# One raw mask buffer in each mask chain, and two places for its additions, in an eight-core two-layer kernel

## The chip, the cores and the metric

The kernel runs on the 8 cores of one Trainium2 chip. Each core works on its own 2048 of the 16384 tokens; the cores exchange nothing, and each reads the whole of the weights and of the mask. The metric is the device time in microseconds of the slowest core. Lower is better.

## The reference

x has shape (2, 8192, 4096). Both weights are 4096 by 4096, and the mask is 4096 by 4096 of int32.

```python
block_mask = mask.reshape(128, 32, 128, 32).astype(float32).sum(axis=(1, 3)) > 0
elem_mask  = repeat(repeat(block_mask, 32, axis=0), 32, axis=1)
x = x + layernorm(einsum('bsk,nk->bsn', layernorm(x), w1 * elem_mask))
x = x + layernorm(einsum('bsi,oi->bso', layernorm(x), sign(w2)) + bias)
```

So the 64 MB mask is reduced to one bit for each block of 32 by 32 weights, and these bits decide which blocks of the first weight matrix count.

## The kernel before

**Chunks and layers.** A core's 2048 tokens are worked on in four chunks (c = 0 to 3) of 512, each in 4 tiles of 128. For each chunk both layers follow one another. Each layer is 16 weight slabs (sl = 0 to 15): slab sl holds half of the contraction (kh = sl % 2) for 512 output features (nsl = sl // 2), 16 pieces of 128 by 512. TensorE multiplies a slab with 64 matmuls into 4 PSUM banks (line 456), and after each odd slab the result is copied out to ARAW.

**The first chunk prepares the weights.** Only in chunk 0 the float32 weights are read, eight pieces of 512 KB for each slab, by SyncE's queue into the two staging buffers WST (line 346). In layer 0 VectorE multiplies each piece with the block bits BTE and writes it as bfloat16 to the slab buffer WSL (line 375). In layer 1 ScalarE takes the sign (line 389). Each finished slab, 2 MB, is written by a DMA of GpSimd's queue to a cache in HBM (c1m and c2m, line 400). The chunks 1 to 3 read the slabs from these caches.

**The mask chain.** `emit_mask_chain(nsl, first)` makes the bits for the two slabs of one nsl; it runs 8 times, all in chunk 0. It has these steps:

- GpSimd (POOL) issues four loads of 128 rows of the mask, 2 MB each (line 230). The numbers of the rows run on over all chains, and even ones go to OS (the output buffer, not in use yet), odd ones to the first half of XP (a buffer that is used after layer 0). Load r + 1 is issued before the wait for load r.
- For each load it adds neighbours pairwise five times (line 250): 2048, 1024, 512, 256 and 128 sums for each partition, the large one out of OS or XP, all of them into the scratch tile MHI. After each addition it waits for its own semaphore. The last 128 sums of each r go to their own part of MHI, at 3072 and up.
- ScalarE converts these 4 x 128 sums into COLRED (line 264), TensorE sums over 32 partitions with a small matmul (line 274), VectorE compares with zero (line 288), TensorE transposes, and VectorE copies the bits into BT (line 292).
- GpSimd writes BT to HBM (line 305) and reads it back, spread over the partitions, into BTE with four DMAs (line 314).

**The order around it.** All engines run their instructions in the order in which the program emits them. The chains 0 and 1 stand ahead of the statistics of the first activation tiles. In layer 0 of chunk 0 the order for each sl is: the load and masking of slab sl + 1 (with the cache write on GpSimd, which waits for the masking), the matmuls of slab sl, and, when sl is even, the chain sl // 2 + 2. So on VectorE the comparison of chain 2 stands behind the masking of slab 1 and ahead of that of slab 2, and chain 3 stands between slabs 3 and 4.

Of the kernel before, what the change touches and what calls it, by code (L numbers as in the profile page):

```python
# [16 lines left out]
I32 = mybir.dt.int32  # L17
AF = mybir.ActivationFunctionType
# [19 lines left out]
def build():  # L38
# [5 lines left out]
    mask_d = nc.dram_tensor("mask", [D, D], I32, kind="ExternalInput")  # L44
# [10 lines left out]
    with es:  # L55
        def sb(name, shape, dt):
            return es.enter_context(nc.sbuf_tensor(name, shape, dt))
# [4 lines left out]
        XP = sb("XP", [128, NT * D], BF16)  # L62
# [4 lines left out]
        MHI = sb("MHI", [128, 3584], I32)  # L67
        COLRED = sb("COLRED", [128, 512], BF16)
# [17 lines left out]
        sem = {n: es.enter_context(nc.semaphore(n)) for n in SEMS}  # L86
        cnt = {n: 0 for n in SEMS}

        def inc(ins, n, k=1):
            cnt[n] += k  # L90
            ins.then_inc(sem[n], k)
            return (n, cnt[n])

        def wt(eng, marker):
            if marker is None:
                return
            n, v = marker
            if v > 0:
                eng.wait_ge(sem[n], v)
# [3 lines left out]
        OSi32 = OS[:, :].bitcast(I32)  # L103
# [112 lines left out]

        def emit_mask_chain(nsl, first):
            halv = {}

            @blk.gpsimd  # L220
            def _(g):
                stg = [OSi32, XP[:, 0:8192].bitcast(I32)]
                ld = {}

                def issue(r):
                    rt = nsl * 4 + r
                    if rt == 0:
                        wt(g, bias_os_free)
                    sn = "sM" if rt % 2 == 0 else "sM1"
                    g.dma_start(stg[rt % 2][:, 0:4096],  # L230
                                mask_d[rt * 128:(rt + 1) * 128, :]
                                ).then_inc(sem[sn], 16)
                    cnt[sn] += 16
                    ld[r] = (sn, cnt[sn])

                issue(0)
                for r in range(4):
                    rt = nsl * 4 + r
                    if r + 1 < 4:
                        issue(r + 1)  # L240
                    wt(g, ld[r])
                    if r == 0 and nsl > 0:
                        g.wait_ge(sem["vAs"], nsl)
                    spans = [(0, 2048), (2048, 1024), (0, 512), (2048, 256),
                             (3072 + r * 128, 128)]
                    cur = stg[rt % 2][:, 0:4096]
                    for hstep in range(5):
                        dst_off, dst_n = spans[hstep]
                        a = cur.rearrange("p (a two) -> p a two", two=2)
                        ins = g.tensor_tensor(MHI[:, dst_off:dst_off + dst_n],  # L250
                                              a[:, :, 0], a[:, :, 1], op=OP.add)
                        m = inc(ins, "vPs", 1)
                        g.wait_ge(sem["vPs"], m[1])
                        cur = MHI[:, dst_off:dst_off + dst_n]
                halv[nsl] = ("vPs", cnt["vPs"])

            conv = {}

            @blk.scalar
            def _(s):  # L260
                wt(s, halv[nsl])
                if nsl >= 1:
                    s.wait_ge(sem["vTp"], 5 * (nsl - 1) + 1)
                ins = s.activation(COLRED[:, :], MHI[:, 3072:3584], AF.Identity)  # L264
                conv[nsl] = inc(ins, "vAs", 1)

            @blk.tensor
            def _(t):
                wt(t, conv[nsl])
                if first:  # L270
                    wt(t, bias_ptB_free)
                if nsl >= 1:
                    t.wait_ge(sem["vMk"], 2 * (nsl - 1) + 1)
                ins = t.matmul(ptB[0:4, 0:512], P4T[:, :], COLRED[:, :],  # L274
                               start=True, stop=True)
                inc(ins, "vTp", 1)
                t.wait_ge(sem["vMk"], 2 * nsl + 1)
                for r in range(4):
                    ins = t.transpose(ptB[:, :].bitcast(BF16)[:, 1024 + r * 4:
                                                              1028 + r * 4],  # L280
                                      BRT[0:4, r * 128:(r + 1) * 128],
                                      IDN[0:4, 0:4])
                    inc(ins, "vTp", 1)

            @blk.vector
            def _(v):
                v.wait_ge(sem["vTp"], 5 * nsl + 1)
                ins = v.tensor_scalar(BRT[0:4, :], ptB[0:4, 0:512], 0.0, None,  # L288
                                      OP.is_gt)
                inc(ins, "vMk", 1)  # L290
                v.wait_ge(sem["vTp"], 5 * nsl + 5)
                ins = v.tensor_copy(BT[:, 16 * nsl:16 * nsl + 16],
                                    ptB[:, :].bitcast(BF16)[:, 1024:1040])
                inc(ins, "vMk", 1)

            res = {}

            @blk.gpsimd
            def _(g):
                g.wait_ge(sem["vMk"], 2 * nsl + 2)  # L300
                g.wait_ge(sem["sB"], cnt["sB"])
                if nsl >= 2:
                    wt(g, bte_freed[nsl - 2])
                bteb = BTE[nsl % 2]
                g.dma_start(btd_d[:, :], BT[:, 16 * nsl:16 * nsl + 16]
                            ).then_inc(sem["sB"], 16)
                cnt["sB"] += 16
                g.wait_ge(sem["sB"], cnt["sB"])
                for a in range(4):
                    out_ap = bass.AP(bteb[:, :].tensor, 32 * a * 512,  # L310
                                     [[512, 32], [16, 32], [1, 16]])
                    in_ap = bass.AP(btd_d[:, :].tensor, a * 16,
                                    [[0, 32], [64, 32], [1, 16]])
                    g.dma_start(out_ap, in_ap).then_inc(sem["sB"], 16)
                    cnt["sB"] += 16
                res["m"] = ("sB", cnt["sB"])

            bte_ready[nsl] = res["m"]
# [469 lines left out]
        for c in range(NCH):  # L788
            t0 = c * TC
            if c == 0:  # L790
                emit_p0_part1(0, list(range(NT)), phase="loads")
                emit_mask_chain(0, True)
                emit_mask_chain(1, False)
                emit_p0_part1(0, list(range(NT)), phase="stats")
            else:
                emit_p0_part1(c, [1, 2, 3])
# [3 lines left out]
            for layer in range(2):  # L800
# [21 lines left out]
                for sl in range(NSL):  # L822
                    if sl + 1 < NSL:
                        nxt = emit_w_load_prep(c, layer, sl + 1)
                    if layer == 0 and fin_pending[0] is not None:
                        fc, fev = fin_pending[0]
                        if sl == 0:
                            fin_chain[0] = emit_finalize_chain(fc, fev)
                        elif sl == 1:
                            for ftt in range(NT):  # L830
                                emit_finalize_tile(fc, fin_chain[0], ftt)
                            fin_pending[0] = None
                    ready, su = pend
                    emit_slab_mm(c, layer, sl, ready, su, ev_at, ht_mark, site,
                                 pre_tt=pre_tt if sl == 0 else None)
                    if c == 0 and layer == 0 and sl % 2 == 0 and sl // 2 + 2 <= 7:
                        emit_mask_chain(sl // 2 + 2, False)
                    if layer == 1 and sl == 8 and c + 1 < NCH:
                        emit_p0_part1(c + 1, [0])
                    if sl + 1 < NSL:  # L840
                        pend = nxt
# [52 lines left out]
```

## Time and profile before

| what | value |
|---|---|
| median of 3 runs (lowest to highest) | 3411.86 us (3408.38 to 3417.56) |
| the profiled execution's own time | 3400.95 us |
| its span, core 2, the slowest | 3399.4 us |
| spans of all cores | 3362.9 to 3399.4 us |
| mean granted TensorE clock, core 2 | 0.818 |
| busy: TensorE matmul, VectorE, ScalarE, GpSimd | 59%, 24%, 18%, 10% |
| share of POOL in the chain of work that ended last | 8% |
| additions of the mask tree, 32 large and 128 small | 115 us and 125.9 us |
| DMA on GpSimd's queue, on SyncE's queue | 194.08 MB, 377.51 MB |

The span is the time from the first to the last instruction of the slowest core in one profiled execution. A share of busy time is a mean over the whole span, although the kernel has stages with different limits: GpSimd's work lies all before about 1000 us, the matmul-heavy chunks 1 to 3 behind it. A chain of work that ended last is followed back from the last instruction, at each step to what released it.

### The profile page before, as it was taken

The numbers are of one execution on the slowest core, as the hardware profiler recorded it, in microseconds if no ns is written. First come the engines' busy times: TensorE is split into PE (matmuls) and PEld (weight loads), VectorE is DVE, ScalarE is ACT, GpSimd is POOL, SyncE is SP. The second block draws the span as 40 slices with busy tenths as digits, with TensorE's granted clock in tenths as the row PEclk, the third lists the DMA queues.
The fourth block names the chain that finished last, engine by engine and source line by source line (L and its number), as shares of the span: only waits on it lengthen the run. The fifth ranks groups of instructions, "written<-read, shape, count | busy, mean of one in ns | idle before, by whom it ended". The sixth has DMA issues, their size and how long they took to land.

```text
span 3399.4 us, 24072 instructions; the slowest of 8 cores (3362.9 to 3399.4 us)
## 1 busy us (share of the span) xinstructions
PE 2016.0 (59%) x9091; PEld 934.2 (27%) x9272; DVE 806.5 (24%) x1300; ACT 607.4 (18%) x460; POOL 343.1 (10%) x328
## 2 busy tenths in 40 slices
PE   1033113332524555555894799579569966965992
PEld 0011001110212222222342344234234432433441
DVE  0132112221440111024013222320222142022214
ACT  0120000000044333332114200301340030115000
POOL 4404432244000000000000000000000000000000
PEclk9986566665866777777997899789779978987996
DMA  3465556555734777664444343443424444342442
GB/s 124 130 205 195 192 210 224 184 187 184 232 133 161 228 230 234 228 217 149 173 152 146 117 180 149 149 173 149 148 107 159 181 149 173 149 148 75 153 160 108
DMA packets 72946, 573.14 MB, mean 169 GB/s; under 512 B 8800, under 2 KB 8816, under 8 KB 42112
## 3 DMA queue, kind: packets, MB, share of 16 engines
q1 hardware_dynamic: 54144, 377.51, 32.6%
q0 software_dynamic: 18688, 194.08, 15.9%
q8 instruction: 75, 1.23, 0.1%
q14 instruction: 39, 0.32, 0.0%
HBM read 470.86 MB, written 100.70 MB: 168 GB/s over the span
## 4 chain that ended last, share of the span: by engine, by line
PE 38%; DMA 28%; DVE 11%; ACT 10%; POOL 8%; issue 5%; DVEq 0%; SPq 0%; POOLq 0%; ACTq 0%
PE pmm L456 36%; DMA WST<-w2s 10%; DMA WST<-w1s 8%; POOL MHI L250 7%; DMA OS<-mask 3%; DMA out<-OS 3%; DVE WSL L375 2%; ACT WSL L389 2%; DMA XS<-x 2%; ACT HS L720 2%; ACT HS L689 2%; DVE OS L768 2%; ACT HT L214 1%; DVE BNST L575 1%; PE ptA L204 1%
## 5 line engine op out<-in xcount | busy, mean ns | idle before, releaser
L456 PE MATMUL pmm<-WSL,HT 128*128 128x512 bf16 x8011 | 1886.5, 397 | 446.3 <-ACT WSL L389 202.0
L456 PEld LDWEIGHTS pmm<-WSL,HT 128*128 128x128 bf16 x8192 | 826.3, 101 | 1497.2 <-issue 617.6
L512 DVE TENSOR_TENSOR ARAW<-pmm,BIASF 128x512 bf16<-128x512 f32 x128 | 88.3, 692 | 898.5 <-PE pmm L456 898.5
L274 PE MATMUL ptB<-COLRED,P4T 128*4 128x512 bf16 x8 | 4.7, 586 | 499.6 <-ACT COLRED L264 499.6
L204 PE MATMUL ptA<-IDN,HS 128*128 128x128 bf16 x576 | 64.7, 302 | 351.4 <-ACT HS L720 236.4
L375 DVE TENSOR_TENSOR WSL<-WST,BTE 128x1024 bf16<-128x1024 f32 x128 | 155.6, 1224 | 208.6 <-DMA WST<-w1s 207.1
L493 DVE BATCH_NORM_STATS2 BNST<-ARAW 128x6 f32<-128x512 bf16 x96 | 59.3, 680 | 533.8 <-ACT ARAW L483 533.8
L389 ACT ACTIVATE WSL<-WST 128x1024 bf16<-128x1024 f32 x128 | 134.7, 1056 | 258.8 <-DMA WST<-w2s 258.5
L204 PEld LDWEIGHTS ptA<-IDN,HS 128*128 128x128 bf16 x576 | 56.6, 140 | 364.7 <-issue 364.0
L264 ACT ACT_TABLE_LOAD x8 | 10.3, 1283 | 741.5 <-POOL MHI L250 741.5
L274 PEld LDWEIGHTS ptB<-COLRED,P4T 128*4 128x4 bf16 x8 | 0.6, 80 | 504.0 <-issue 504.0
L250 POOL TENSOR_TENSOR MHI<-MHI 128x1024 int32<-128x1024 int32 (+3 forms) x128 | 125.9, 984 | 18.3
L657 POOL DMA_DIRECT2D XS<-x x32 | 22.5, 703 | 1016.5 <-DVE XP L682 948.3
L214 ACT ACTIVATE HT<-ptA 128x2048 bf16<-128x2048 bf16 x36 | 67.6, 1877 | 274.2 <-PE ptA L204 274.2
L575 DVE BATCH_NORM_STATS2 BNST<-XS 128x6 f32<-128x512 f32 x128 | 78.4, 679 | 149.2 <-DMA XS<-x 149.2
L288 DVE TENSOR_SCALAR BRT<-ptB 4x512 bf16<-4x512 f32 x8 | 5.4, 679 | 433.7 <-PE ptB L274 433.7
L483 ACT ACTIVATE ARAW<-pmm 128x512 bf16<-128x512 f32 x96 | 57.3, 597 | 269.7 <-PE pmm L456 153.1
L483 ACT ACT_TABLE_LOAD x24 | 30.8, 1283 | 394.6 <-PE pmm L456 394.6
L519 DVE BATCH_NORM_STATS2 BNST<-ARAW 128x6 f32<-128x512 bf16 x160 | 98.9, 681 | 4.1
L544 POOL DMA_DIRECT2D XS<-x x24 | 12.7, 528 | 612.5 <-ACT HS L609 563.0
L768 DVE SCALAR_TENSOR_TENSOR OS<-XP,AUX,OS 128x4096 f32<-128x4096 bf16 x16 | 71.8, 4485 | 1.7
L250 POOL TENSOR_TENSOR MHI<-OS 128x2048 int32<-128x2048 int32 x16 | 57.6, 3601 | 109.6 <-DMA OS<-mask 109.5
(58 smaller groups left out, 807.7 us busy)
## 6 DMA issues: line engine op xcount, KB each, us to landing
WSL<-c1m SPq DMA_DIRECT2D x48, 2048.0 KB, 8.0
WSL<-c2m SPq DMA_DIRECT2D x48, 2048.0 KB, 8.0
WST<-w1s SPq DMA_DIRECT2D x128, 512.0 KB, 5.0
WST<-w2s SPq DMA_DIRECT2D x128, 512.0 KB, 4.7
XS<-x POOLq DMA_DIRECT2D x56, 1024.0 KB, 6.3
OS<-mask POOLq DMA_DIRECT2D x16, 2048.0 KB, 10.3
XP<-mask POOLq DMA_DIRECT2D x16, 2048.0 KB, 12.4
c1m<-WSL POOLq DMA_DIRECT2D x16, 2048.0 KB, 10.3
```

Of the source, the lines that this page charges most:

```text
L204: ins = t.transpose(pt[:, j * 128:(j + 1) * 128], HS[:, ktg * 128:(ktg + 1) * 128], IDN[:, :])
L214: ins = eng.activation(dst, src, AF.Identity)
L250: ins = g.tensor_tensor(MHI[:, dst_off:dst_off + dst_n], a[:, :, 0], a[:, :, 1], op=OP.add)
L375: ins = v.tensor_tensor(dst, src, mk, op=OP.mult)
L389: ins = s.activation(buf[:, j0 * 512:(j0 + KTQ) * 512], WST[(wfirst + q) % 2][:, :], AF.Sign)
L456: ins = t.matmul(acc_bank(use8, nsl, tt), st_ap, mv_ap, start=(kh == 0 and j == 0), stop=(kh == 1 and j == KTS - 1))
L483: ins = s.activation(dst, acc_bank(use8, nsl, tt), AF.Identity)
L512: ins = v.tensor_tensor(dst, acc_bank(use8, nsl, tt), BIASF[:, nsl * 512:(nsl + 1) * 512], op=OP.add)
L519: ins = v.bn_stats(BNST[:, sslot * 48 + nsl * 6: sslot * 48 + (nsl + 1) * 6], ARAW[:, tt * D + nsl * 512: tt * D + (nsl + 1) * 512])
L575: ins = v.bn_stats(bn[:, (hf * 4 + q) * 6: (hf * 4 + q + 1) * 6], xb[:, q * 512:(q + 1) * 512])
L689: ins = s.activation(HS[:, :], XP[:, tt * D:(tt + 1) * D], AF.Square, accum_out=XSQ[:, tt:tt + 1])
L768: ins = v.scalar_tensor_tensor(OS[:, :], XP[:, tt * D:(tt + 1) * D], mrs3, OS[:, :], OP.subtract, OP.add)
```

## The change

Within one chain all four loads now go to the same raw buffer: OS for even nsl, the first half of XP for odd nsl. A load is issued after the first (large) addition of the row block before it has finished, no longer before the wait for it. The sums of odd chains go to the second half of XP, and those of even chains to MHI. GpSimd's wait for ScalarE's conversion is for that of two chains before, and starts with chain 2. Sizes and number of all loads and additions are the same.

```diff
--- before.py
+++ after.py
@@ -216,42 +216,49 @@
 
         def emit_mask_chain(nsl, first):
             halv = {}
+            par = nsl % 2
+            XPI = XP[:, :].bitcast(I32)
+            if par == 0:
+                raw = OSi32[:, 0:4096]
+                tree = MHI
+                fin_base = 3072
+            else:
+                raw = XPI[:, 0:4096]
+                tree = XPI[:, 4096:8192]
+                fin_base = 3072
+            spans_tpl = [(0, 2048), (2048, 1024), (0, 512), (2048, 256)]
 
             @blk.gpsimd
             def _(g):
-                stg = [OSi32, XP[:, 0:8192].bitcast(I32)]
                 ld = {}
 
                 def issue(r):
                     rt = nsl * 4 + r
                     if rt == 0:
                         wt(g, bias_os_free)
-                    sn = "sM" if rt % 2 == 0 else "sM1"
-                    g.dma_start(stg[rt % 2][:, 0:4096],
-                                mask_d[rt * 128:(rt + 1) * 128, :]
+                    sn = "sM" if par == 0 else "sM1"
+                    g.dma_start(raw, mask_d[rt * 128:(rt + 1) * 128, :]
                                 ).then_inc(sem[sn], 16)
                     cnt[sn] += 16
                     ld[r] = (sn, cnt[sn])
 
                 issue(0)
                 for r in range(4):
-                    rt = nsl * 4 + r
-                    if r + 1 < 4:
-                        issue(r + 1)
                     wt(g, ld[r])
-                    if r == 0 and nsl > 0:
-                        g.wait_ge(sem["vAs"], nsl)
-                    spans = [(0, 2048), (2048, 1024), (0, 512), (2048, 256),
-                             (3072 + r * 128, 128)]
-                    cur = stg[rt % 2][:, 0:4096]
+                    if r == 0 and nsl >= 2:
+                        g.wait_ge(sem["vAs"], nsl - 1)
+                    spans = spans_tpl + [(fin_base + r * 128, 128)]
+                    cur = raw
                     for hstep in range(5):
                         dst_off, dst_n = spans[hstep]
                         a = cur.rearrange("p (a two) -> p a two", two=2)
-                        ins = g.tensor_tensor(MHI[:, dst_off:dst_off + dst_n],
+                        ins = g.tensor_tensor(tree[:, dst_off:dst_off + dst_n],
                                               a[:, :, 0], a[:, :, 1], op=OP.add)
                         m = inc(ins, "vPs", 1)
                         g.wait_ge(sem["vPs"], m[1])
-                        cur = MHI[:, dst_off:dst_off + dst_n]
+                        if hstep == 0 and r + 1 < 4:
+                            issue(r + 1)
+                        cur = tree[:, dst_off:dst_off + dst_n]
                 halv[nsl] = ("vPs", cnt["vPs"])
 
             conv = {}
@@ -261,7 +268,9 @@
                 wt(s, halv[nsl])
                 if nsl >= 1:
                     s.wait_ge(sem["vTp"], 5 * (nsl - 1) + 1)
-                ins = s.activation(COLRED[:, :], MHI[:, 3072:3584], AF.Identity)
+                ins = s.activation(COLRED[:, :],
+                                   tree[:, fin_base:fin_base + 512],
+                                   AF.Identity)
                 conv[nsl] = inc(ins, "vAs", 1)
 
             @blk.tensor
```

## Rows read from the trace of the kernel before

**Rows 1.** Chain of work that ended last, first 900 us, by line.

```profile
by line: DMA WST<-w1s 28.1%; POOL MHI L250 27.0%; DMA OS<-mask 12.9%; DVE WSL L375 8.1%; issue 7.1%; DMA XS<-x 2.3%; PE ptB L137 1.7%; DVE BNST L575 1.3%; ACT L264 1.1%; DVE ARAW L510 1.1%; DMA OS<-bias 0.9%; DVE BNST L519 0.9%; ACT HS L609
```

**Rows 2.** Waits, first 900 us: waiter, releaser, total us, times, longest.

```profile
ACT L264 <- POOL MHI L250: 741.5, 8, 106.6
...
POOL MHI L250 <- DMA OS<-mask: 109.5, 8, 16.5
```

**Rows 3.** POOL's time line, chain 2, last large addition: start, duration.

```profile
245.96 0.55 POOL L400 DMA_DIRECT2D c1m<-WSL  x1 [26.73 <-DVE WSL L375]
246.51 0.54 POOL L230 DMA_DIRECT2D OS<-mask  x1
247.03 0.53 POOL L230 DMA_DIRECT2D XP<-mask  x1
261.93 3.59 POOL L250 TENSOR_TENSOR MHI<-OS 128x2048 int32<-128x2048 int32 x1 [14.37 <-DMA OS<-mask]
265.67 4.36 POOL L250 TENSOR_TENSOR MHI<-MHI 128x1024 int32<-128x1024 int32 x4
270.59 0.55 POOL L230 DMA_DIRECT2D OS<-mask  x1 [0.56 <-POOL MHI L250]
271.15 3.61 POOL L250 TENSOR_TENSOR MHI<-XP 128x2048 int32<-128x2048 int32 x1
...
288.71 3.60 POOL L250 TENSOR_TENSOR MHI<-XP 128x2048 int32<-128x2048 int32 x1 [0.20 <-POOL MHI L250]
292.45 4.36 POOL L250 TENSOR_TENSOR MHI<-MHI 128x1024 int32<-128x1024 int32 x4
...
820.68 3.60 POOL L250 TENSOR_TENSOR MHI<-XP 128x2048 int32<-128x2048 int32 x1 [0.20 <-POOL MHI L250]
```

**Rows 4.** VectorE's time line behind chain 2.

```profile
299.82 0.68 DVE L288 TENSOR_SCALAR BRT<-ptB 4x512 bf16<-4x512 f32 x1 [54.42 <-PE ptB L274]
...
301.32 2.36 DVE L375 TENSOR_TENSOR WSL<-WST,BTE 128x1024 bf16<-128x1024 f32 x2
```

**Rows 5.** Issues by time (to 812 us): KB each, us to landing.

```profile
OS<-mask POOLq DMA_DIRECT2D x1, 2048.0 KB, 10.9
...
XP<-mask POOLq DMA_DIRECT2D x1, 2048.0 KB, 16.3
...
OS<-mask POOLq DMA_DIRECT2D x1, 2048.0 KB, 8.7
...
OS<-mask POOLq DMA_DIRECT2D x1, 2048.0 KB, 12.2
...
OS<-mask POOLq DMA_DIRECT2D x1, 2048.0 KB, 8.1
...
c1m<-WSL POOLq DMA_DIRECT2D x1, 2048.0 KB, 10.2
...
c1m<-WSL POOLq DMA_DIRECT2D x1, 2048.0 KB, 11.3
...
OS<-mask POOLq DMA_DIRECT2D x1, 2048.0 KB, 15.2
...
XP<-mask POOLq DMA_DIRECT2D x1, 2048.0 KB, 19.6
...
OS<-mask POOLq DMA_DIRECT2D x1, 2048.0 KB, 9.6
...
OS<-mask POOLq DMA_DIRECT2D x1, 2048.0 KB, 14.3
...
OS<-mask POOLq DMA_DIRECT2D x1, 2048.0 KB, 17.1
...
XP<-mask POOLq DMA_DIRECT2D x1, 2048.0 KB, 8.3
```

**Rows 6.** Busy time by engine, chain 2 and after 1735 us.

```profile
core 2: us, PE busy (x) PEld busy (x) DVE busy (x) ACT busy (x) POOL busy (x), PEclk, DMA share, GB/s
246.51:307.55 61.04, 7.49 (x27) 2.94 (x28) 4.43 (x5) 1.91 (x2) 36.00 (x30) 0.52 0.54 199
1735.00:3399.00 1664.00, 1281.47 (x5985) 605.51 (x6105) 426.30 (x748) 298.79 (x213) 24.03 (x38) 0.88 0.39 146
```

## The prediction

> **What bounds the kernel now.** I compared the spans of the cores first: they lie within 1.1% of each other, so this is no matter of one core. Then I read the chain of work that ended last, cut to the first 900 us [rows 1]: 27.0% of that stretch is the mask tree on POOL (line 250) and 12.9% are mask loads; the reader should see that the mask chain, although it only prepares a small bit table, is as large a part of that path as the weight loads. The waits of the same stretch say who is held up [rows 2]: ScalarE stood 741.5 us in 8 waits for the last tree step, and POOL itself stood 109.5 us in 8 waits, one for each chain, all for the chain's first load. The time line of POOL for chain 2 shows the rhythm [rows 3]: two loads are issued at 246.51 and 247.03, the first addition (3.59 us) starts at 261.93, the four small ones (4.36 us from first to last end) at 265.67, the next load is issued at 270.59 and the next first addition starts at 271.15. So three periods take 288.71 - 261.93 = 26.78 us, 8.9 us each, and no load after the first is waited for by more than a trace.
>
> Why does all of it reach the end? VectorE, in program order, has this chain's comparison ahead of the masking of the next weight slab. It stood idle 54.42 us before the comparison at 299.82 and began that slab's multiplication at 301.32 [rows 4]. Behind that multiplication is the slab's write to the cache, behind that (POOL, in order) the next slab's, and behind that the next chain's first load at 351.21, which closes the loop. ScalarE has nothing but the chain there, and TensorE is busy only 7.49 of 61.04 us [rows 6]. SP has its two staging buffers loaded already and can go no further. So no engine has work that a longer chain could cover: a microsecond more in a chain is a microsecond more in the span. Chains 0 and 1, before the loop, are followed on VectorE by the statistics of the first activation tile, which need only the loads of x that landed long before; they are exposed as well. Thus 8 chains count, each in full.
>
> The landing times of single DMAs come from the view of DMA issues, asked for one short stretch each [rows 5]. In order they are: chain 0, first, second and third load; chain 1, first and third; the cache writes at 218.66 (no mask load behind it) and 245.96 (with two); chain 2, first and second load; chain 3, third; chain 5, first; chain 7, first and fourth.
>
> **The change, part by part.**
>
> *One raw buffer in a chain instead of two.* The order of additions, their sizes and their number (160) stay; their operands move, and 3.60 and 3.61 us for the large addition out of OS or XP say that a buffer's place costs nothing. What goes is the early issue: a load is now issued only when the first addition of the row before has emptied the only buffer. Counting from the start T of a first addition: it ends at T + 3.6; the issue follows 0.56 us later (the idle time before each DMA issue behind an addition, 270.59 in [rows 3]), at T + 4.17; the load lands L later; the next first addition starts about 0.18 us after a landing (246.51 + 15.22 = 261.73, then 261.93). The small additions, about 0.55 us of issue and 4.6 us with their waits, end near T + 9.3 and lie inside the load. The period becomes 4.35 + L.
>
> For L the trace has 16 loads in the same situation (third and fourth of each chain, with the queue otherwise empty): 8.1 to 9.6 us, mean 8.53; the first (8.7), the last (8.3), the shortest and the longest of the 16 stand in [rows 5]. They too had additions running on POOL while they landed. So the period becomes 12.88 us, three of them 38.6 us in place of 26.8: **+11.86 us a chain, +94.9 us for 8**. The ends: L = 8.1 gives 3 x 12.45 - 26.78 = 10.6 (84.6 in all), L = 9.6 gives 15.1 (120.6).
>
> *The second load is no longer in flight beside the first.* This is a gain. In chain 0 nothing else is in flight, and the first load lands after 10.9 us [rows 5], against 8.5 for one alone: 2.4 us back; chain 1 (12.2 us) I count alike. In chains 2 to 7 the first load lands after 14.3 to 17.1 us, 15.5 on the mean of the six (15.2 in chain 2; the shortest and the longest stand there too), and it stands behind the cache write of 2 MB issued 0.55 us before it, which lands after 11.3 us in chain 2 and is still there after the change. The spacing of landings, 15.2 and then 19.6 + 0.52 = 20.1 us, is that of three transfers one behind another; the one taken away is the last. Bounds: nothing (pure order of issue, the last holds nobody up) and 4.9 us (its whole spacing, if the three share evenly). The cache writes with mask loads behind them (11.3 us) against one without (10.2 us at 218.66) differ by about 1 us, nearer to nothing than to 4.9; between this and 2.4 I take 1.5. Gain: 2 x 2.4 + 6 x 1.5 = **-13.8 us**, bounds 0 and -34.
>
> *The trees' two places, and the wait for ScalarE's conversion of two chains before instead of one.* Worth nothing: POOL cannot start a chain before VectorE's comparison of the chain before, which already stands behind that conversion. The first issue of a chain is not moved: it still stands behind the former chain's four BTE copies and the cache write. So the second buffer frees no one. Cost 0; with its cover gone, still at most the 0.2 us of a semaphore.
>
> Sum: +94.9 - 13.8 = **+81 us**. On the profiled execution's 3400.95 us that is 3482 us; its span is 1.6 us less, and the median of the three runs is 3411.86, 11 us above it. Since that is what is compared, I add to the median: **3493 us**, +2.4%.
>
> A rule beside it: the Trainium skill, "DMA: Bandwidth & Descriptors", section "Anatomy of one DMA — SWDGE (gpsimd) path", fits such a transfer as about 2.0 us plus its bytes over 436 GB/s. For 2 MB that would be an estimate of 6.8 us, and by it the change would gain about 10 us in all instead of costing 81. The trace has no mask load under 8.1 us with eight cores loading at once, and the measured duration is used.
>
> **The rivals.**
>
> *A. Loads alone land much sooner (other side).* With landing L for all four, a chain costs 3 x (4.35 + L) + L; before it cost 26.8 + 15.4 = 42.2 in chains 2 to 7. They meet at L = 7.3 us; below it the kernel gets faster. Landings behind one another come 4.9 to 5.9 us apart [rows 5], so the data alone could move in 5.9: then 36.7 us, -5.5 in six chains, -1.0 and -2.3 in the first two, **3375 us**. For it: less is in flight on all cores. Against: 16 of 16 loads that had the queue to themselves took 8.1 or more. The skill's fit, cited above, is this rival's milder form, about 3402 us.
>
> *B. The first load drops to 8.5 us in all chains*, because the mask pair and not the cache write delays it: -7.0 in six chains and -2.4 in chain 0, -3.7 in chain 1; 94.9 - 48 = +47, **3459 us**. For it: the landing of 10.9 falls to the 8.5 of a lone load without any write. Against: the cache write, landing after 11.3 us, is issued first on the same queue.
>
> *C. Loads land more slowly than now*, because descriptor work on POOL now meets four short additions instead of one long one: L = 10.9, the slowest first load without a write, gives 3 x 15.25 - 26.8 = +19, 8 x 19 - 14 = +138, **3550 us**. Against: today's loads are followed by the same short additions 3.7 us later and land in 8.1 to 9.6 us.
>
> *D. The clock gives it back.* After 1735 us TensorE is busy 1281.5 us at a granted clock of 0.88 [rows 6], a mix of its levels of 1.2 and 2.4 GHz. To win 81 us there the clock would have to be 6.3% higher, about 0.94 on the mean; **3412 us**, within noise. Against: the extra idle time lies before 900 us, and what TensorE does just before this stretch is the same.
>
> **How the numbers follow.** Forecast 0.80, with its own range of 3468 to 3520; A 0.03, of which a third lands within the noise; B 0.10; C 0.04; D 0.03. Bounds of the unknown costs: low 84.6 - 34 = +51, high +120 without any gain; the high end needs L = 9.6, the longest of the 16, in all 24 loads, so I stop at +108 us. The range of 3460 to 3520 takes in B's edge and nearly all of the forecast. About 0.3% (10 us) is what a measurement of this kernel can tell from no change. Faster: 0.02 from A and 0.01 from D; within: 0.03 from A and D; slower: 0.94.
>
> **What would show it.** In the changed kernel's profile: POOL's time line has, in each chain, issue after the large addition and not before it; idle time of about 3.5 us, released by the mask load, before the second, third and fourth large addition (24 such waits, some 85 us in all, where there was next to nothing); periods near 12.9 us; mask loads with a median near 8.5 us; a first load of about 8.5 us in chain 0 and 14 us in chains 2 to 7; the last large addition, which starts at 820.68 now, some 80 us later, and all that follows it as long as before. It is wrong if the landings alone differ from 8.5 (3 us of span per 0.125 us), if the first load gains more than 1.5 us, or if what follows the last mask chain changes its length.

## The result, and the profile of the changed kernel

The changed kernel takes **3484.4 us** (median of 10 runs, 3475.5 to 3499.4) against 3415.9 us for the kernel before (10 runs, 3400.8 to 3420.6): a ratio of **1.0213**, 95% interval 1.0191 to 1.0234, thus slower by 65 to 80 us. The forecast was +81 us on the median, 3493 us. Of the kernels below some executions ran more than 1.5% over the others, with a lower granted clock on one die or both: the ratios leave these out, the medians and ranges count them.

The profiled execution has a span of 3488.8 us on core 1, 89 us above the span before. The profiled execution before lay 15 us under its median and this one 6 us above, so the two traces are further apart than the medians.

The chain of work that ended last, cut to the first 1000 us:

```profile
by line: DMA WST<-w1s 24.2%; DMA OS<-mask 16.1%; DMA XP<-mask 16.0%; DVE WSL L384 7.4%; POOL XP L255 7.4%; POOL MHI L255 7.4%; issue 6.3%; DMA XS<-x 2.1%; DVE ARAW L519 1.7%; PE ptB L137 1.5%; DVE BNST L528 1.4%; DVE BNST L584 1.2%; ACT L27
```

Against [rows 1], the mask loads went from 12.9% of 900 us (116 us) to 32.1% of 1000 us (321 us), and the additions from 27.0% (243 us) to 14.8% (148 us). The work is the same, but now the small additions lie beside a load. That is how a lost overlap looks in this view: what was hidden and what was exposed change places.

GpSimd's time line, chain 2 (start, duration; in brackets the idle time before and what ended it), which answers to [rows 3]:

```profile
267.24 0.56 POOL L409 DMA_DIRECT2D c1m<-WSL  x1 [26.65 <-DVE WSL L384]
267.79 0.53 POOL L240 DMA_DIRECT2D OS<-mask  x1
284.67 3.59 POOL L255 TENSOR_TENSOR MHI<-OS 128x2048 int32<-128x2048 int32 x1 [16.35 <-DMA OS<-mask]
288.85 0.55 POOL L240 DMA_DIRECT2D OS<-mask  x1 [0.59 <-POOL MHI L255]
289.42 4.38 POOL L255 TENSOR_TENSOR MHI<-MHI 128x1024 int32<-128x1024 int32 x4
297.76 3.60 POOL L255 TENSOR_TENSOR MHI<-OS 128x2048 int32<-128x2048 int32 x1 [3.96 <-DMA OS<-mask]
...
310.54 3.60 POOL L255 TENSOR_TENSOR MHI<-OS 128x2048 int32<-128x2048 int32 x1 [3.69 <-DMA OS<-mask]
...
323.02 3.60 POOL L255 TENSOR_TENSOR MHI<-OS 128x2048 int32<-128x2048 int32 x1 [3.38 <-DMA OS<-mask]
```

Each large addition after the first is now held up by its load for 3.4 to 4.0 us, and the three periods take 323.02 - 284.67 = 38.35 us, where they took 26.78. On this core the 24 waits of this kind add up to 87 us. The first load, though no second mask load is in flight with it now, is waited for 16.35 us, not less than the 14.37 us before (and 0.53 us of the second issue).

The busy times of the engines before and behind the last cache write of the first layer (kernel before, then changed kernel; us, PE, PEld, DVE, ACT, POOL, granted clock, DMA share, GB/s):

```profile
0.00:936.00 936.00, 276.41 (x1126) 120.62 (x1147) 227.56 (x276) 47.91 (x33) 299.32 (x256) 0.74 0.58 188
936.00:3399.40 2463.40, 1739.61 (x7966) 813.55 (x8125) 578.95 (x1024) 559.47 (x427) 43.80 (x73) 0.85 0.45 161
```

```profile
0.00:1022.00 1022.00, 278.49 (x1147) 120.59 (x1148) 227.74 (x276) 47.95 (x33) 299.93 (x257) 0.73 0.53 172
1022.00:3488.80 2466.80, 1759.31 (x8126) 815.29 (x8124) 579.10 (x1024) 560.17 (x427) 42.57 (x72) 0.84 0.46 161
```

86 of the 89 us lie ahead of that write; the rest of the kernel is 3 us longer, at a granted clock of 0.84 instead of 0.85. Every engine is as busy as before: nothing became slower, it only waits more. (TensorE's 20 us more behind the write come with 160 more recorded matmuls; the trace before lacks some. GpSimd is not idle behind the write either, as "all before about 1000 us" would have it: its 43.8 us there are DMA issues.)

The same reading on all eight cores, from their GpSimd time lines (means over cores and chains, us):

| kernel | issue of first load to first addition: chain 0, chain 1, chains 2 to 7 | three periods | last cache write |
|---|---|---|---|
| before | 9.9, 10.6, 15.6 | 27.0 | 928.9 |
| changed | 9.7, 9.0, 15.5 | 38.5 | 1017.5 |

The mean span of the eight cores grew from 3380.7 to 3470.9 us between the two profiled executions, by 90 us.

### The profile page after: what moved, and what is told of

Same layout as the page of the kernel before. It is cut to its first block, busy times and chain, and to the rows that moved or that the text cites. A ratio compares the mean times of both kernels' runs of the same rounds, so it can differ in the third digit from the quotient of the medians.

```text
span 3488.8 us, 24252 instructions; the slowest of 8 cores (3456.6 to 3488.8 us)
## 1 busy us (share of the span) xinstructions
PE 2037.8 (58%) x9272; PEld 935.9 (27%) x9272; DVE 806.8 (23%) x1300; ACT 608.1 (17%) x460; POOL 342.5 (10%) x328
## 3 DMA queue, kind: packets, MB, share of 16 engines
q8 instruction: 75, 1.23, 0.1%
## 4 chain that ended last, share of the span: by engine, by line
PE 37%; DMA 33%; DVE 11%; ACT 10%; POOL 4%; issue 4%; DVEq 0%; SPq 0%; ACTq 0%; POOLq 0%
PE pmm L465 35%; DMA WST<-w2s 10%; DMA WST<-w1s 7%; DMA OS<-mask 5%; DMA XP<-mask 5%; DMA out<-OS 3%; DVE WSL L384 2%; POOL XP L255 2%; POOL MHI L255 2%; ACT WSL L398 2%; DMA XS<-x 2%; ACT HS L729 2%; ACT HS L698 2%; DVE OS L777 2%; ACT HT L214 1%
## 5 line engine op out<-in xcount | busy, mean ns | idle before, releaser
L465 PE MATMUL pmm<-WSL,HT 128*128 128x512 bf16 x8192 | 1908.0, 398 | 440.0 <-ACT WSL L398 203.6
L271 ACT ACT_TABLE_LOAD x8 | 10.3, 1283 | 823.7 <-POOL MHI L255 415.6
L255 POOL TENSOR_TENSOR XP<-XP 128x2048 int32<-128x2048 int32 (+4 forms) x80 | 120.6, 1508 | 109.0 <-DMA XP<-mask 101.3
```

The costliest lines, as they stand in the source:

```text
L255: ins = g.tensor_tensor(tree[:, dst_off:dst_off + dst_n], a[:, :, 0], a[:, :, 1], op=OP.add)
L465: ins = t.matmul(acc_bank(use8, nsl, tt), st_ap, mv_ap, start=(kh == 0 and j == 0), stop=(kh == 1 and j == KTS - 1))
```

## The experiments

Their times stand beside runs of the kernel before on the same chip; ratios are to these.

**The second place for the sums, alone.** The kernel before with its two raw buffers, and with the change's other part:

```diff
+        trees = [MHI, XP[:, :].bitcast(I32)[:, 4096:8192]]
...
-                    if r == 0 and nsl > 0:
-                        g.wait_ge(sem["vAs"], nsl)
+                    if r == 0 and nsl >= 2:
+                        g.wait_ge(sem["vAs"], nsl - 1)
...
-                        ins = g.tensor_tensor(MHI[:, dst_off:dst_off + dst_n],
+                        ins = g.tensor_tensor(tree[:, dst_off:dst_off + dst_n],
...
```

> The kernel before, with two raw buffers and the early issue kept, and only the change's second part: sums of odd chains in the second half of XP, and the wait for the conversion two chains back. My theory (a chain cannot start before the comparison of the chain before, so the second place frees no one): within 10 us of before, three periods stay at 27.0 us. Rival (the place of the sums costs or gives something): additions out of XP into XP of other than 3.60 us, and a time off by more than 10 us.

Measured: 3403.1 us, ratio 0.9988 (0.9951 to 1.0024); three periods 27.0 us, last cache write at 922.9. No difference that can be told: this half of the change is worth nothing while the chains cannot overlap, as the prediction had it.

**Late issue, but two buffers.**

```diff
-                    if r + 1 < 4:
-                        issue(r + 1)
...
                         g.wait_ge(sem["vPs"], m[1])
+                        if hstep == 0 and r + 1 < 4:
+                            issue(r + 1)
```

> The kernel before with both raw buffers in turn and one place for the sums, but each load issued only after the first addition of the row block before. My theory (the lateness of the issue is the whole cost, not the sharing of a buffer): as the changed kernel, three periods of 38.5 us and about 70 to 90 us over before. Rival (a load into the very buffer that was just read is what is slow): clearly less than the changed kernel, three periods under 35 us.

Measured: 3481.9 us, ratio 1.0219 (1.0154 to 1.0284); three periods 38.2 us, last cache write at 1007.0. The time line of its slowest core, where the raw buffer alternates:

```profile
284.76 0.55 POOL L230 DMA_DIRECT2D XP<-mask  x1 [0.59 <-POOL MHI L248]
285.33 4.38 POOL L248 TENSOR_TENSOR MHI<-MHI 128x1024 int32<-128x1024 int32 x4
293.18 3.60 POOL L248 TENSOR_TENSOR MHI<-XP 128x2048 int32<-128x2048 int32 x1 [3.47 <-DMA XP<-mask]
```

The load goes to the buffer that nobody reads, and the addition still waits 3.47 us for it. So the moment of the issue makes the whole loss. The single buffer is only what forces it.

**The second load held back.** This tests the prediction's gain of 13.8 us by itself.

```diff
-                    if r + 1 < 4:
+                    if 0 < r < 3:
                         issue(r + 1)
                     wt(g, ld[r])
+                    if r == 0:
+                        issue(1)
```

> The kernel before, but the second load of each chain is issued only when the first has landed, before the first addition. The prediction's sizes (the second load delays the first by 2.4 us in two chains and 1.5 us in six) give first additions 1.5 to 2.4 us sooner after the first issue. The changed kernel's trace says otherwise (waits before the first addition of chains 2 to 7 15.5 us as before): then the first load lands when it did, and the later period grows by the issue, 0.6 to 1.5 us a chain, so +5 to +12 us in all against -14 + 8 = -6 us by the prediction's sizes.

Measured: 3412.3 us, ratio 0.9993 (0.9961 to 1.0025); from the first issue to the first addition 10.3, 10.2 and 17.0 us (chain 0, chain 1, chains 2 to 7), of which 0.9 is the second issue, now in between; three periods 26.9 us; last cache write 928.3.

```profile
242.21 0.53 POOL L230 DMA_DIRECT2D OS<-mask  x1
258.25 0.53 POOL L230 DMA_DIRECT2D XP<-mask  x1 [15.52 <-DMA OS<-mask]
258.80 3.61 POOL L252 TENSOR_TENSOR MHI<-OS 128x2048 int32<-128x2048 int32 x1
```

With no second load at all in flight, the wait for the first is 15.52 us. The second load does not delay the first in chains 2 to 7 (17.0 less 0.9 is 16.1 us, against 15.6 before), and the gain of 1.5 us a chain was not there to be had. In chains 0 and 1, where no write is ahead, 9.4 and 9.3 us are left after taking off the 0.9, against 9.9 and 10.6 before: 0.5 and 1.3 us on the mean instead of 2.4. The cores show more than the mean. In chain 0 they stand in two groups before: the first load lands after 8.3 to 8.6 us on the cores 1, 3 and 5 and after 10.1 to 11.0 us on the others. With the second load held, landings of 8.2 to 10.6 us remain, four of them over 9, and in the changed kernel 8.2 to 11.0, so the 10.9 us that the prediction read on core 2 is for the most part not the second load's doing. What puts a core into the late group is open; before and with the load held, each of the pairs of cores 0 and 1, 2 and 3, 4 and 5 has one of each. In chain 1 the second load does matter on the late cores: 12.0 to 12.3 us with it, 9.6 to 9.9 without, while the others land after 8.1 to 8.9 us either way. The loss that I expected in the time did not show: the 1.4 us more until the first addition of chains 2 to 7 met shorter stretches between the chains (48.3 us against 49.5).

**The first load ahead of the cache write.**

```diff
...
                     wt(g, ready)
+                    if layer == 0 and kh == 1 and sl <= 11:
+                        mn = (sl + 3) // 2
+                        g.dma_start(OSi32[:, 0:4096],
+                                    mask_d[mn * 512:mn * 512 + 128, :]
+                                    ).then_inc(sem["sM"], 16)
...
```

> The kernel before, but in the six chains of the loop the first mask load is issued just ahead of the 2 MB cache write of the odd slab instead of just behind it. Theory: the cache write ahead of it, and not the second mask load behind it, is what makes the first load take 15.5 us; then the first addition starts about 11 us after the issue instead of 15.5, and the kernel is some 20 to 30 us faster. Rival: all that is in flight shares evenly, the order does not matter, and the wait stays above 14 us and the time within 10 us.

Measured: the first addition comes 11.8 us after the issue instead of 15.6, as the theory says, but the three periods grew from 27.0 to 28.6 us, and the last cache write came at 917.6, 11 us earlier than before. The time is 3410.2 us, ratio 0.9995 (0.9971 to 1.0020), which does not show these 11 us and misses the 20 to 30 that I expected. The mean span over the cores is shorter, 3376.0 us against 3383.2 us; that of the slowest core, which the metric takes, is not (3410.4 and 3409.1 us on the mean of the executions).

```profile
248.77 0.56 POOL L406 DMA_DIRECT2D OS<-mask  x1 [28.58 <-DVE WSL L380]
249.32 0.53 POOL L412 DMA_DIRECT2D c1m<-WSL  x1
249.84 0.53 POOL L232 DMA_DIRECT2D XP<-mask  x1
261.46 3.59 POOL L255 TENSOR_TENSOR MHI<-OS 128x2048 int32<-128x2048 int32 x1 [11.08 <-DMA OS<-mask]
...
271.49 3.59 POOL L255 TENSOR_TENSOR MHI<-XP 128x2048 int32<-128x2048 int32 x1 [0.83 <-DMA XP<-mask]
```

Order on the queue decides who waits: 3.8 us less for the first load in six chains (-23 us), given back in good part by the second load, which is now the one behind the write (8 x 1.6 = +13 us). The write ahead makes 3.8 of the 6.9 us by which the first load's 15.6 exceed a lone load's 8.7. The other 3.1 us were not taken apart: the write and the second load now follow, and a weight load of 512 KB, issued at 248.25 in this trace, is in flight and lands after 8.0 us.

**The changed kernel with the next chain's first load issued early.** Its second raw buffer is idle while the other is in use, so the load can be issued behind the last large addition of the chain before.

```diff
-                issue(0)
+                if nsl == 0:
+                    issue(0)
+                else:
+                    ld[0] = early.pop(nsl)
...
+                        if hstep == 0 and r == 3 and nsl + 1 < 8:
...
+                            g.dma_start(nraw, mask_d[nrt * 128:(nrt + 1) * 128, :]
+                                        ).then_inc(sem[sn], 16)
...
```

> The changed kernel, and in addition the first load of chain n + 1 is issued into the other raw buffer as soon as the last large addition of chain n is done. If the first wait is exposed in full (theory), 6 waits of 15.5 us and one of 9 us go: 102 us less than the changed kernel, about 3380 us, 30 to 35 us less than before. Rival (the wait for the first load is hidden behind the cache write or comes back at the second load): less than 50 us won back, above 3430 us.

Measured: 3404.6 us, ratio 0.9988 (0.9962 to 1.0014), 80 us less than the changed kernel and even with the one before, so the 30 to 35 us below it did not come; last cache write at 931.3 instead of 1017.5. The first additions now start right behind the cache write's issue. Of the 102 us expected, 17 came back in the periods (40.6 instead of 38.5 us in 8 chains: the second load now is the one behind the write) and 7 as one more issue in each chain. So with the next chain's load issued early, the changed layout wins back what it costs, and no more.

**All loads two row blocks ahead, with the buffers of the kernel before.**

```diff
...
-                    if r + 1 < 4:
-                        issue(r + 1)
-                    wt(g, ld[r])
+                    wt(g, ld[rt])
...
                         g.wait_ge(sem["vPs"], m[1])
+                        if hstep == 0 and rt + 2 < 32:
+                            issue(rt + 2)
```

> The kernel before, with each load issued two row blocks ahead, over the ends of the chains too (the buffer is free after the large addition two blocks before). If the first wait is exposed in full, 10.6 + 6 x 15.6 = 104 us go and one issue of 0.9 us comes in each chain: about 3315 us. Rival: the loads come back as contention with the weight loads or the cache writes between the chains: above 3350 us.

Measured: **3315.7 us**, ratio 0.9714 (0.9678 to 0.9749). Three periods take 27.9 us, the last cache write comes at 840.2, 89 us earlier. The forecast from the exposed waits was 97 us less; the ratio says 98, and the last cache write 89, so the agreement of the time is closer than that of its parts. A wait read on this path is worth nearly its full length: the waits taken away were read as 104 us, the longer periods give back 7, and 89 show at the last cache write.

```profile
244.03 0.55 POOL L402 DMA_DIRECT2D c1m<-WSL  x1 [29.90 <-DVE WSL L377]
244.60 3.61 POOL L250 TENSOR_TENSOR MHI<-OS 128x2048 int32<-128x2048 int32 x1
248.80 0.55 POOL L230 DMA_DIRECT2D OS<-mask  x1 [0.59 <-POOL MHI L250]
```

**The additions between the slabs.** On top of the last one, the additions of chains 2 to 7 go in halves behind each cache write, a slab earlier than they stood, and the rest of the chain one slab later:

```diff
-                    if c == 0 and layer == 0 and sl % 2 == 0 and sl // 2 + 2 <= 7:
-                        emit_mask_chain(sl // 2 + 2, False)
+                    if c == 0 and layer == 0 and sl <= 11:
+                        if sl % 2 == 0:
+                            if sl // 2 + 2 <= 7:
+                                emit_mask_rows(sl // 2 + 2, [2, 3])
+                        else:
+                            emit_mask_rest((sl + 3) // 2, False)
+                            if (sl + 3) // 2 + 1 <= 7:
+                                emit_mask_rows((sl + 3) // 2 + 1, [0, 1])
...
```

> As the kernel with loads two row blocks ahead, and the additions of chains 2 to 7 are cut in two halves of two row blocks, one behind each cache write, a slab ahead of where they stood, so that they run while VectorE masks the next slab; conversion, sums and comparison stand one slab later. Theory (a chain is exposed only by its place in the order): the 6 chains of the loop cost their comparison alone, and the first layer of the first chunk is bound by its weight loads: 3100 to 3220 us. Rival (the mask loads, 8 MB for each two slabs, slow the weight loads and the masking by as much as they hide): above 3280 us, with slab times well over 30 us.

Measured: **3250.2 us**, ratio 0.9521 (0.9481 to 0.9562), the fastest of the kernels that leave nothing out; last cache write at 771.9. It lies between the two forecasts, 30 us above the theory's range and 30 below the rival's. A pair of slabs takes 86 us (288.60 to 374.64 between cache writes), against 104.7 us before (245.96 to 350.67), but the 43 us for each slab are the rival's sign. Two further kernels say what fills them.

**Without the additions, and without the loads.**

```diff
-                    cur = stg[rt % 2][:, 0:4096]
-                    for hstep in range(5):
+                    few = rt >= 8
+                    cur = stg[rt % 2][:, 0:256 if few else 4096]
+                    for hstep in ([4] if few else range(5)):
...
```

> The kernel with the additions between the slabs, but in chains 2 to 7 only the last small addition of each row block is left (128 sums of the first 256 values of the loaded row block), so the block bits are not those of the mask; all loads stay. Its time tells what POOL's additions cost while VectorE masks. In the kernel with the additions VectorE's busy time is 63 us above that of before, from maskings of up to 6.2 us instead of 1.23. Theory A (the two engines' additions and multiplications hinder one another, and that is on the path): VectorE's busy time back to 807 us and 40 us or more off 3250 us. Theory B (the loads hold it, the stretched maskings only fill VectorE's waits): within 15 us of 3250 us.

```diff
-                    wt(g, ld[rt])
+                    wt(g, ld.get(rt))
...
-                        if hstep == 0 and rt + 2 < 32:
+                        if hstep == 0 and rt + 2 < 8:
```

> The kernel with the additions between the slabs, but from chain 2 on no mask is loaded: the additions run on the rows that chain 1 left, so the bits are not those of the mask. 48 MB less is read. Theory B (loads hold it): 1.2 MB less for each 5 us of weights, slab pairs fall from 87 us to about 60 us, and the kernel to 3080 to 3130 us. Theory A: VectorE's busy time stays near 869 us and the kernel above 3200 us.

Measured: without the additions 3228.0 us, ratio 0.9453 (0.9420 to 0.9486), some 23 us less; without the loads 3138.8 us, ratio 0.9192 (0.9146 to 0.9238), some 112 us less, with slab pairs of about 62 us. Both times lie outside both theories' ranges: 23 us is more than B's 15 and less than A's 40, and 3138.8 us is 9 above B's 3130. The loads hold the kernel for the most part, and the two engines hinder one another for a smaller one. A kernel without both was not run, so whether the two parts add up is open. The masking instruction in the kernel with both, without additions and without loads (busy, mean ns; idle before), on the slowest core of each:

```profile
L379 DVE TENSOR_TENSOR WSL<-WST,BTE 128x1024 bf16<-128x1024 f32 x128 | 218.5, 1719 | 334.0 <-DMA WST<-w1s 332.3
```

```profile
L380 DVE TENSOR_TENSOR WSL<-WST,BTE 128x1024 bf16<-128x1024 f32 x128 | 156.4, 1228 | 377.4 <-DMA WST<-w1s 376.1
```

```profile
L379 DVE TENSOR_TENSOR WSL<-WST,BTE 128x1024 bf16<-128x1024 f32 x128 | 255.7, 2015 | 180.4 <-DMA WST<-w1s 178.9
```

62 us of stretched maskings shorten VectorE's waits by 43 us, so only 19 us, about a third of them, should be seen in the time, and 23 are. Take the loads away, and the wait for weights falls from 332 to 179 us.

## Why the prediction was right, and where it was not

- **The chain is exposed in full.** Right. The last cache write of the first layer moved by 88.6 us on the mean of the cores; the terms below add up to 91.8 - 2.1 - 2.5 = 87.2, the last being slightly shorter stretches between chains (49.5 to 49.0 us, five of them). Loads issued ahead then removed the first waits, too, at nearly their full length. On the mean of the cores it holds to the end as well (+90 us of span), but not quite on the slowest core, which the metric takes.
- **+11.86 us a chain for the late issue, 94.9 in all.** Right: 38.49 - 27.02 = 11.47 us, 91.8 in all. The period of 4.35 + L with L = 8.53 gave 12.88 and was 12.83. That this is so close is partly luck: 8.53 us was the mean on core 2, while the same 16 loads took 8.85 us on the mean of all cores, 7.9 to 11.2 singly, which would have forecast +100 us. In the changed kernel lone loads became a little shorter, 8.5 us for the 24 loads of each core. The late issue with two buffers, at the same periods and time, shows that it is the issue and not the shared buffer.
- **-13.8 us for the first load.** This term was mis-sized: it measured 0.2 us in chain 0, 1.5 in chain 1 and 0.05 in each of the other six, about 2 us in all. What failed is the step "between this and 2.4 I take 1.5", and for chain 0 the reading of 10.9 us on one core as the second load's doing. On the cores 1, 3 and 5 the first load's addition already followed after 8.5 to 8.7 us before the change, with a second load in flight; I had read one core only. The held second load shows it directly for the loop's chains: 15.5 us of wait with no mask load behind it. That the write ahead makes more than half of what this wait has over a lone load was shown by the swapped order (11.8 us). The prediction's lower bound, order of issue alone, was the right value there; in chain 1 the second load did cost the late cores some 2.4 us, as the prediction had it.
- **0 for the two places and the relaxed wait.** Right: ratio 0.9988 with only this part.
- **The sum.** By the two measured terms (91.8 - 2.1) it should have been about +90, and it was 86 us at the last cache write and 89 in the span between the two profiled executions. The medians say +68.5, the ratio +73. That the forecast of +81 lies between is luck in part, two misses that lean opposite ways: the first-load term was 12 us too generous, and the time of the slowest core grew by some 17 to 21 us less than the terms say.
- **Mean core and slowest core.** About ten of these us lie in the metric. In 35 executions of the kernel before, on three chips, the mean span over the cores is 3377.5 to 3385.3 us by the chip, and the slowest core lies 25 to 27 us above it. In 11 executions of the changed kernel the mean is 3468.9 us, and the slowest core lies 15 us above it. So the mean core lost 84 to 91 us, as the terms say, and the slowest only 72 to 81. The traces point the same way: of each pair of cores (0 and 1, 2 and 3, 4 and 5, 6 and 7) the later one's last cache write moved by 84 us on the mean, the earlier one's by 93. Why the cores of a pair lie closer together after the change was not tested, and the rest of the difference is open.
- **The rivals.** A (lone loads much quicker) fell: the landings of chain 2 below. The Trainium skill, "DMA: Bandwidth & Descriptors", section "Anatomy of one DMA — SWDGE (gpsimd) path", fits 2.0 us plus bytes over 436 GB/s, by estimate 6.8 us for 2 MB; no mask load of either trace lands before 7.9 us, with all eight cores loading. (By the prediction's own terms that fit would gain 8 us, not about 10.) B fell: chains 2 to 7 still waited 15.5 us. C fell with the same landings: with the short additions behind each issue, the 24 loads of a core landed after 8.5 us on the mean of the cores. D fell: behind the first layer's last write the kernel is 3 us longer, at a clock 0.01 lower.

The four loads of chain 2 in the changed kernel (view of DMA issues, one stretch each; the last figure is us from issue to landing), against those of [rows 5]:

```profile
OS<-mask POOLq DMA_DIRECT2D x1, 2048.0 KB, 16.7
...
OS<-mask POOLq DMA_DIRECT2D x1, 2048.0 KB, 8.8
...
OS<-mask POOLq DMA_DIRECT2D x1, 2048.0 KB, 8.5
...
OS<-mask POOLq DMA_DIRECT2D x1, 2048.0 KB, 8.2
```


## What to carry to other kernels

A double buffer earns what its early issue hides, and that can be read ahead of time: period without it = (first read + issue + landing), period with it = the larger of compute and landing (here 12.8 and 8.9 us); then ask how many of these periods are on the path. A second buffer for the results was worth nothing here, because program order puts the whole of one step behind the whole of the other: move the first instruction of the next step first. For the delay that one transfer gives another, look at the order on the queue and at several cores before you take a number from one.

## What the runs showed of the hardware

- **A load behind a write of the same queue pays for the write, and a second load behind both costs it nothing.** A 2 MB load issued 0.55 us behind a 2 MB write could be used after 15.6 us with a second load behind it and after 15.5 us without one, and after 11.8 us when it was issued ahead of the write. Lone loads landed after 8.1 to 9.6 us on core 2 and 7.9 to 11.2 us over all cores. Without a write ahead a second load is not free: in chain 1 it made 12.0 to 12.3 us out of 9.6 to 9.9 on half of the cores.
- **Integer additions on GpSimd and multiplications on VectorE stretch one another.** The multiplication of 128 x 1024, 1.23 us alone, took up to 6.2 us beside them (mean 1.72, and 2.02 in the kernel without mask loads), and four small additions took up to 6.9 us instead of 4.4. With the additions gone and the loads kept, the mean multiplication is back at 1.23 us. VectorE's lines at such a place, and GpSimd's:

```profile
294.42 2.36 DVE L379 TENSOR_TENSOR WSL<-WST,BTE 128x1024 bf16<-128x1024 f32 x2
301.17 6.20 DVE L379 TENSOR_TENSOR WSL<-WST,BTE 128x1024 bf16<-128x1024 f32 x1 [4.39 <-DMA WST<-w1s]
```

```profile
299.51 3.14 POOL L318 DMA_DIRECT2D BTE<-btd  x4 [4.01 <-DMA btd<-BT]
302.67 3.61 POOL L251 TENSOR_TENSOR MHI<-OS 128x2048 int32<-128x2048 int32 x1
306.87 0.59 POOL L231 DMA_DIRECT2D OS<-mask  x1 [0.59 <-POOL MHI L251]
307.48 5.19 POOL L251 TENSOR_TENSOR MHI<-MHI 128x1024 int32<-128x1024 int32 x4
```

The masking that starts at 301.17 ends at 307.37, behind the large addition's end at 306.28.
